# A graph attention layer on one core: more source rows fetched one by one from SyncE and ScalarE

## The reference

```python
Q, K, V = x @ Wq + bq, x @ Wk + bk, x @ Wv + bv       # (6250, 96) each
Eh = edge_attr @ We + be                               # (100000, 96)
s = (K[src] * Q[dst] / sqrt(12) * Eh).reshape(-1, 8, 12).sum(-1)
s = exp(clip(s, -5, 5))                                # one weight per edge and head
wV = segment_sum(V[src] * s, dst); Z = segment_sum(s, dst)
out = layernorm(x + wV / (Z + 1e-6))
```

## Time and profile before

| | |
|---|---|
| median of 3 runs | 993.1 us (992.93 to 993.73) |
| profiled execution | 993.86 us, span 992.1 us |
| busy in the span | GpSimd 74%, VectorE 66%, TensorE 65%, ScalarE 19% |
| mean granted clock of TensorE | 0.81 |

### The profile page before, as it was taken

How to read it: one execution, slowest core, us unless ns; L and a number is a source line. 1 busy time by engine, 2 the same in 40 slices (tenths; PEclk the granted TensorE clock), 3 DMA queues, 4 the chain that set the end, 5 groups by cost and what they waited for, 6 DMA issues and landing times. The chain is left out here.

```text
span 992.1 us, 15976 instructions
## 1 busy us (share of the span) xinstructions
PE 643.3 (65%) x3276; PEld 419.8 (42%) x3276; DVE 653.0 (66%) x1307; ACT 189.4 (19%) x378; POOL 737.3 (74%) x778
## 2 busy tenths in 40 slices
PE   6778777766566766666557656664675566657563
PEld 5655555444343434344334434443343344334342
DVE  6638987877666675766566656664775566657655
ACT  4842211111111111111111111111111111111111
POOL 7777777777777777777777777777777777777772
PEclk9888988788877777778777877788788878777876
DMA  6999776666655557656565665565665655664531
GB/s 201 311 285 241 185 188 184 188 173 172 176 147 168 150 140 185 165 138 175 143 173 150 164 177 149 139 177 145 168 170 145 180 147 137 177 176 123 145 80 47
DMA packets 103482, 165.77 MB, mean 167 GB/s; under 512 B 46285, under 2 KB 66126, under 8 KB 103375
## 3 DMA queue, kind: packets, MB, share of 16 engines
q1 hardware_dynamic: 64399, 84.88, 31.3%
q0 software_dynamic: 36544, 74.37, 28.4%
q10 hardware_dynamic: 2432, 5.41, 1.6%
HBM read 152.19 MB, written 12.39 MB: 166 GB/s over the span
## 5 line engine op out<-in xcount | busy, mean ns | idle before, releaser
L424 POOL DMA_INDIRECT kv<-kv_table,idx x740 | 703.7, 951 | 225.6 <-issue 224.3
L527 PE MATMUL psT<-identity,qe 96*128 96x96 f32 x782 | 115.3, 307 | 242.7 <-DVE qe L872 242.6
L955 DVE TENSOR_TENSOR qke<-psT,kv 128x768 f32<-128x768 f32 (+1 forms) x99 | 93.6, 945 | 266.5 <-DMA kv<-kv_table,idx 257.2
L506 PE MATMUL psE<-ea,we 97*96 97x512 f32 x392 | 259.7, 799 | 0.8 <-ACT kv L646 0.8
L527 PEld LDWEIGHTS psT<-identity,qe 96*128 96x128 f32 x782 | 93.2, 178 | 259.8 <-DVE qe L872 259.7
L576 PE MATMUL psA<-place,msg 128*104 128x104 f32 x1536 | 170.1, 266 | 22.4 <-DVE msg L982 22.1
L576 PEld LDWEIGHTS psA<-place,msg 128*104 128x104 f32 x1536 | 160.1, 180 | 51.2 <-DVE msg L982 45.0
L676 ACT ACTIVATE qe<-psE 96x1024 f32<-96x1024 f32 (+1 forms) x99 | 99.8, 1008 | 217.2 <-PE psE L506 217.2
L872 DVE TENSOR_TENSOR qe<-psQ,qe 96x1024 f32<-96x1024 f32 (+1 forms) x99 | 118.4, 1196 | 7.8 <-ACT qe L676 7.8
L506 PEld LDWEIGHTS psE<-ea,we 97*96 97x96 f32 x392 | 75.9, 219 | 80.2 <-issue 80.2
L690 ACT ACTIVATE msg<-clipped 128x64 f32<-128x64 f32 (+1 forms) x99 | 25.3, 255 | 419.8 <-DVE clipped L970 413.8
(11 more groups left out here) (105 smaller groups left out, 349.5 us busy)
## 6 DMA issues: line engine op xcount, KB each, us to landing
ea<-eaT SPq DMA_DIRECT2D x99, 384.0 KB, 4.0
q_parts<-rel_table SPq DMA_DIRECT2D x99, 252.0 KB
kv<-kv_table,idx POOLq DMA_INDIRECT x740
q_full<-kv_table SPq DMA_DIRECT2D x640, 0.8 KB
q_full<-kv_table ACTq DMA_DIRECT2D x640, 0.8 KB
qwin<-q_table SPq DMA_DIRECT2D x198, 23.6 KB
xb<-xrows SPq DMA_DIRECT2D x24, 144.0 KB
out<-ob SPq DMA_DIRECT2D x24, 144.0 KB
```

What stands on the lines that cost most here:

```text
L424: pool.indirect_dma_start(kv[:, k, t], None, kv_table, sources).then_inc(kv_in[k], 16)
L506: last = nc.tensor.matmul(psE[0:D, h, 0:size], we[:], ea[:, k % EAR, edge:edge + size], start=True, stop=True)
L527: last = nc.tensor.transpose(psT[:, t % 2, t // 2 * D:(t // 2 + 1) * D], qe[0:D, k % 2, t * P:(t + 1) * P], identity[0:D, 0:D])
L955: nc.vector.tensor_tensor(qke[:, 0:nt].rearrange("p (t b) d -> p b t d", **by_bank), psT[:, :, 0:nt // 2 * D].rearrange("p b (t d) -> p b ...
```

## The change

Seventeen tiles in place of ten come row by row. SyncE fetches six tiles (groups 18, 31, ... 83) with 10 rows a turn, in two batches of five; ScalarE fetches eleven (groups 13, 21, ... 93) with 16 rows a turn, in two batches of eight. Each batch has its own register load. ScalarE's batches stay where its one batch was in a turn, behind the copy of a due tile. The window bases are loaded without their range assertions.

```diff
-SP_ROWS, ACT_ROWS = 8, 8
+SP_ROWS, ACT_ROWS = 10, 16
+SP_STEP, ACT_STEP = 5, 8
 SP_TURNS, ACT_TURNS = -(-P // SP_ROWS), -(-P // ACT_ROWS)
 FROM = 4
-SP_TILES = tuple(22 + SP_TURNS * i for i in range(5))
-ACT_TILES = tuple(23 + ACT_TURNS * i for i in range(5))
+SP_TILES = tuple(18 + SP_TURNS * i for i in range(6))
+ACT_TILES = tuple(13 + ACT_TURNS * i for i in range(11))
...
-        def load_single_rows(eng, i, j, rows):
-            count = min(rows, P - j * rows)
-            edge = i * P + j * rows
+        def load_single_rows(eng, i, start, count):
+            edge = i * P + start
...
-                    qbase_int[0:1, bass.ds(2 * g, 2 * count)], engines=[sp.engine], min_val=0, max_val=NR - QW)[1]
+                    qbase_int[0:1, bass.ds(2 * g, 2 * count)], engines=[sp.engine], min_val=0, max_val=NR - QW,
+                    skip_runtime_bounds_check_because="the lowest target node of half a group, at most N")[1]
...
-                            load_single_rows(sp, turn // SP_TURNS, turn % SP_TURNS, SP_ROWS)
+                            start = turn % SP_TURNS * SP_ROWS
+                            for row in range(start, min(P, start + SP_ROWS), SP_STEP):
+                                load_single_rows(sp, turn // SP_TURNS, row, min(SP_STEP, P - row))
...
-                            load_single_rows(act, len(SP_TILES) + turn // ACT_TURNS, turn % ACT_TURNS, ACT_ROWS)
+                            start = turn % ACT_TURNS * ACT_ROWS
+                            for row in range(start, min(P, start + ACT_ROWS), ACT_STEP):
+                                load_single_rows(act, len(SP_TILES) + turn // ACT_TURNS, row, min(ACT_STEP, P - row))
```

More of the change, by code:

```diff
@@ L219, in load_single_rows @@
             for p in range(count):
-                eng.dma_start(kv_rows[j * rows + p:j * rows + p + 1, i], kv_table[bass.ds(nodes[p], 1), :]
+                eng.dma_start(kv_rows[start + p:start + p + 1, i], kv_table[bass.ds(nodes[p], 1), :]
                               ).then_inc(rows_in[i], 16)
```

## The result

The changed kernel takes 1106.5 us (median of 4, 1102.2 to 1109.9) where the kernel before takes 993.4 us: ratio 1.1136, 95% interval 1.1096 to 1.1176. The forecast was slower, 1071 us, 1010 to 1110. The profiled execution took 1109.94 us with a span of 1108.1.

What follows compares the result with a forecast made beforehand. GpSimd's gathers bound the kernel at 39 us a block; ScalarE's loop would overtake them. Span: 98.7 + 22 blocks of 42 (924) + 1.8 + 24 + 20.3 = 1068.8, plus 1.8 around it: 1071 us, range 1010 to 1110.

Steps and rivals of the forecast that it cites:

- ScalarE's second batch is on the path and makes the loop slower than the gathers: ScalarE, VectorE and TensorE loop: added issues lengthen a block of four groups from 30.5 to 42 us, beyond the gathers' 39.
- 4.1 us for a batch, with no other bound: ScalarE, each turn of groups 4 to 91: second register load and eight more row DMAs add 4.1 us.
- First turn: Block's first turn: edge projection evacuation (L676) follows the sums copy after 3.56 or 6.07 us, depending on TensorE's clock.
- the slow case: TensorE's matmuls at half rate behind a longer wait: 40.5 + 2.5 = 43.0 us a block; 42 was taken.
- The range: Whole kernel: 1010 to 1110 us for 8 in 10; the steps' own range, blocks of 39.9 to 43 us, 1024 to 1093.
- Third turn: Block's third turn on ScalarE: L676 of the next turn waits for TensorE anyway, which swallows this batch's 4.1 us.
- Seven gathers less are worth nothing here: GpSimd: 740 gathers become 733, saving 8.8 us, worth nothing because GpSimd no longer sets the pace.
- Tail of 46 us after the last rows: After the last row issues, from the sums copy before group 92 to the end: 1.8 + 24 + 20.3 us.
- SyncE's part and the assertions at nothing: SyncE: two more rows and a second load, 1.7 us a turn, less assertions; lies in its slack, costed at nothing.
- Copies wait for landings: Rival: ScalarE's copies of single tiles wait for late rows, up to 60 us more, 1095 to 1150 us; chance 0.13.
- The rule that issues are light: Skill's rule speaking against the forecast: the moved issues would be light, giving the gather-paced rival's 985 us; chance 0.10.

Runs made afterwards that it cites:

- ScalarE's half alone: Changed kernel with SyncE back to 8 rows a turn, five tiles and one load, ScalarE keeping 16 rows and eleven tiles: 1105.8 us, ratio 1.1107.
- the moved jobs: Changed kernel with the layer norm's two activations ahead of their turn's rows and the copy of the sums between the previous turn's two batches: 997.1 us, ratio 1.0027.
- the copy of the sums moved: Changed kernel with only the copy of the sums moved between the two batches of the turn before: 1000.1 us, ratio 1.0045.
- the run with one load: Changed kernel with ScalarE loading the node numbers of its sixteen rows by one register load instead of two: 1047.3 us, ratio 1.0540.
- the run with all seventeen tiles and one load: Changed kernel with sums copy and layer norm activations moved, one load a turn (ScalarE two of eight in a block's fourth turn): 992.2 us, ratio 0.9989.
- the fourth turn light: Changed kernel with ScalarE issuing 8 rows instead of 16 in each block's fourth turn, nine of its tiles by row: 1004.8 us, ratio 1.0083.

## Why the prediction was right, point by point

- *ScalarE's second batch is on the path and makes the loop slower than the gathers.* Right: shown by ScalarE's half alone (all of the loss), by the moved jobs (110 of 113 us back), and by GpSimd's 128.8 us of waits for queries.
- *4.1 us for a batch, with no other bound.* From L679 to the copy of the sums it is 227.26 - 218.96 = 8.30 us in the block above, where it was 4.13, but 8.3 to 9.2 over the 22 blocks and 8.56 by the mean: 4.4 us for the batch. One part of it is the register load, now 0.77 us by the median and up to 1.32 where it was 0.72. Short by 0.3, three times a block: some 20 us in all.
- *First turn: L676 follows the copy after 3.56 or after 6.07 us, by TensorE's clock; I leaned to the slow case.* It is 6.07 (184.68 to 190.75), and 5.5 to 6.07 in every block after the first. TensorE's timeline of that place shows the wait and the slow projection, 3.62 us as at 129.85:

```profile
185.22 0.79 PE L540 MATMUL psA<-identity,accT 104*128 104x104 f32 x3 [6.41 <-ACT accT L687]
185.81 1.48 PE L530 MATMUL psT<-identity,qe 96*128 96x96 f32 x8
187.09 3.62 PE L509 MATMUL psE<-ea,we 97*96 97x512 f32 x4
```

  I had the slow case worked out at 43.0 us a block and still took 42. Block 43.6 against 42 is the size that was off: 22 x 1.6 = 36 us, nearly all that the forecast was short. 22 us of it are the choice of 42, the other 14 are what 43.0 was short, for which the batch's price is enough. The tail adds 3.3.
- *The range.* The 1106.5 us lie above the 1024 to 1093 that the steps gave. The wide range reached 1110 for two other reasons: copies that wait for landings, which no copy did, and a longer issue, which is the 0.3 us a batch. That it held the result is in part luck.
- *Third turn: its batch is swallowed by the wait for the edge projection.* Right for the time of the block: taking it away gave 9 us, taking the fourth turn's away 105. In the block shown nothing is left to wait for (L679 at 218.96 follows at once), so it is swallowed only up to the time that TensorE takes there.
- *Seven gathers less are worth nothing here.* Right. They are worth their 1.25 us each where gathers set the pace: four of them gave ratio 0.9954, where 5.0 us would be 0.9950.
- *Tail of 46 us after the last rows.* 49.4.
- *SyncE's part and the assertions at nothing.* Right for the time. The reason was too easy: I priced SyncE's second load at 0.9 us with its gap; the median duration of a load rose from 0.77 to 1.33 us, and there are two. At the gathers' pace 108.5 us of its slack are left, about as many as my sum leaves, but only because the missing assertions gave some 45 us back. And a sum of slack says nothing on single tiles, which came up to 12 us late.
- *Copies wait for landings.* In the changed kernel none of the 17 copies waits for its rows. With the copy of the sums moved eight do, 13.6 us in all and up to 2.8. One of them starts at 566.13 after 1.38 us idle, its rows issued until 563.48, so its last row had landed 2.65 us after the last issue; behind SyncE's rows for group 31 above it was 1.46. The 10 us of this rival are far from that. SyncE's tiles were late by their issue.
- *The rule that issues are light.* The Trainium skill ("DMA: Bandwidth & Descriptors", "Issuing engines are not separate DMA queues") calls the sequencer's time for starting a DMA usually small beside the DMA itself. For one row that is so here: 0.40 us of ScalarE's stream (6.34 us for sixteen in the run with one load) against 1.5 to 2.7 us until the last row has landed. But the issues stand one behind the other in ScalarE's stream and other work stands behind them, and a batch more a turn costs 11% of the kernel.

## What to carry to other kernels

An engine that is busy 19% of the time has no spare time as such: ask what stands behind the work you give it, in each kind of turn. The stretch of the trace in which the present bottleneck doesn't bind shows the next loop's own pace; add the new work to it turn by turn, and compare with the bottleneck's. Before dropping such a change, move the short jobs that others wait for ahead of the long ones, and load the registers of a batch at once. A sum of slack on another engine tells what a change costs in total, not whether a single result comes in time.

## What was not expected of the hardware

- A register load on SyncE takes 0.77 us by the median in the kernel before (80 loads of eight numbers) and 1.33 us with two loads of five in a turn (156 loads, up to 1.54); ScalarE's loads of eight went from 0.72 to 0.77. One load of ten in a turn took 1.25 (the run with all seventeen tiles and one load). Fewer numbers took longer than eight, and why isn't settled.
- ScalarE's load of sixteen numbers takes 1.20 us by the median where one of eight takes 0.72: 0.06 us a number over a fixed part. The register loads of the run with one load for sixteen rows, duration in ns min/median/max:

```profile
L216 SPq TENSOR_LOAD <-row_id x156: 523/1328/1462, 94.7 to 872.8; - x156
L216 ACTq TENSOR_LOAD <-row_id x88: 1178/1195/1214, 101.7 to 987.6; - x88
```

- TensorE's mean granted clock fell a little. Over 300 to 900 us (us busy and count by engine, PE, PEld, DVE, ACT and POOL, then granted clock, DMA share, GB/s), after:

```profile
300.00:900.00 600.00, 368.64 (x1741) 248.23 (x1740) 348.24 (x686) 81.81 (x161) 405.59 (x429) 0.76 0.53 143
```

  It was 0.79 before. The two levels, 2.4 and 1.2 GHz, show in the edge projection, 1.88 or 3.62 us for four matmuls: the granted clock was 1.00 at 160.95 to 162.6 in the kernel before and 0.50 at 187.1 to 190.5 after. Behind a wait of 2.82 us the projection was fast, behind that of 6.41 us slow. That pair alone proves little: in the kernel before it was slow, too, at 129.85 and in most later blocks, behind waits of 2.2 to 2.7 us. But behind all 22 waits of 5.5 to 7.3 us in the changed kernel it took 3.1 to 3.6 us, and with the fourth turn light, behind waits of 0.6 to 2.9 us, it was fast, 1.88 us, in 16 blocks of 22. So the longer wait came with a slower projection behind it and cost twice; what decides the level behind a short wait isn't shown.
